# Two attention stages of a kernel: the uses of one shared PSUM bank get other places in the round

## What is computed

```python
x = x + _L0_ffn_ref(_layernorm(x), g_info, W_qkv, W_proj, b_proj)          # "ra": register attention
...
x = x + _L3_xattn_ref(ctx, _layernorm(x), mask, mask, W_src, ..., W_out)   # "ma": masked attention
```

## Time and profile before

| What | Value |
|---|---|
| median of three executions | 2350.74 us |
| the profiled execution, its own time | 2351.17 us |
| its span, granted TensorE clock | 2349.3 us, 0.959 |
| TensorE busy | 2057.0 us (88% of the span) |
| VectorE, ScalarE, GpSimd busy | 1252.7, 1019.3, 300.4 us |
| stage ra, 147 to 380 us of the span | 233.0 us, of it TensorE 212.76, VectorE 158.78, ScalarE 164.79 |
| stage ma, 1810 to 1987 us | 177.0 us, of it TensorE 165.50, VectorE 93.42, ScalarE 83.17 |

### The profile page before, as it was taken

One profiled execution on the slowest core, in us unless ns is written; L12 is line 12 of the kernel. 1 busy time (PEld: TensorE's weight loads), 2 busy tenths in 40 slices (PEclk: granted clock), 3 DMA queues, 4 the chain that ended last, 5 costly groups with the idle time before them and its releaser, 6 DMA issues. The chain is left out here.

```text
span 2349.3 us, 38236 instructions
## 1 busy us (share of the span) xinstructions
PE 2057.0 (88%) x14629; PEld 1545.4 (66%) x14629; DVE 1252.7 (53%) x2505; ACT 1019.3 (43%) x2851; POOL 300.4 (13%) x392
## 2 busy tenths in 40 slices
PE   6789998899997689979999999978998998785795
PEld 4556666566665589766666667657886777663684
DVE  6457665788876144365554455655444555553113
ACT  3247774777775245333333333443222544333122
POOL 0101110222211524200000000031002000001212
PEclk8989999999999889989999999999999999997898
DMA  3000001121212633340000000010002000005352
GB/s 132 18 1 1 1 2 46 28 56 38 58 33 90 234 85 90 99 148 10 10 10 10 1 10 1 1 32 1 1 1 79 28 19 22 1 1 167 126 184 81
DMA packets 92564, 114.79 MB, mean 49 GB/s; under 512 B 20217, under 2 KB 75521, under 8 KB 91489
## 3 DMA queue, kind: packets, MB, share of 16 engines
q1 hardware_dynamic: 87440, 98.75, 13.8%
q0 software_dynamic: 4944, 13.59, 1.6%
HBM read 79.89 MB, written 25.08 MB: 45 GB/s over the span
## 5 line engine op out<-in xcount | busy, mean ns | idle before, releaser
L957 ACT ACTIVATE ca_prob<-bank,ca_nmax 128x512 f32<-128x512 f32 x256 | 174.2, 691 | 73.2 <-DVE ca_nmax L1024 73.2
L1024 DVE TENSOR_REDUCE ca_nmax<-bank 128x1 f32<-128x512 f32 x256 | 164.2, 683 | 40.9 <-PE bank L806 40.9
L957 ACT ACTIVATE na_prob<-bank,na_nmax 128x257 f32<-128x257 f32 x256 | 118.1, 474 | 148.4 <-DVE na_nmax L1024 148.4
L820 PE MATMUL bank<-cst,ca_prob 128*128 128x128 f32 x1024 | 140.6, 278 | 7.6 <-DVE ca_pT L1030 5.9
L820 PEld LDWEIGHTS bank<-cst,ca_prob 128*128 128x128 f32 x1024 | 111.0, 141 | 53.6 <-issue 44.9
L957 ACT ACTIVATE ra_prob<-bank,ra_nmax 128x256 f32<-128x256 f32 x256 | 118.4, 486 | 53.4 <-DVE ra_nmax L1024 53.4
L1024 DVE TENSOR_REDUCE na_nmax<-bank 128x1 f32<-128x257 f32 x256 | 90.9, 418 | 68.7 <-PE bank L806 68.7
L2267 PE MATMUL bank<-sf_h,sf_W 128*128 128x512 f32 x512 | 120.1, 395 | 0.0
L2267 PEld LDWEIGHTS bank<-sf_h,sf_W 128*128 128x128 f32 x512 | 95.9, 187 | 23.5
L2135 PE MATMUL bank<-na_Wkv,na_cxT 128*128 128x512 f32 x224 | 103.6, 605 | 0.0
L1024 DVE TENSOR_REDUCE ra_nmax<-bank 128x2 f32<-128x512 f32 x128 | 82.0, 683 | 39.6 <-PE bank L806 39.6
(11 more groups left out here) (475 smaller groups left out, 4611.9 us busy)
## 6 DMA issues: line engine op xcount, KB each, us to landing
xl_w<-in_L_ffn_w SPq DMA_DIRECT2D x16, 1024.0 KB, 7.6
rf_sent<-rf_w SPq DMA_DIRECT2D x13, 390.0 KB, 6.2
rf_xin<-rf_sent SPq DMA_DIRECT2D x39, 128.0 KB, 2.1
dp_cx<-in_ctx_tok SPq DMA_DIRECT2D x4, 1024.0 KB, 13.8
ca_v<-in_ctx_values SPq DMA_DIRECT2D x8, 512.0 KB, 4.8
rf_W<-in_L_ffn_w SPq DMA_DIRECT2D x8, 512.0 KB, 10.6
rf_rows<-rf_back SPq DMA_DIRECT2D x8, 512.0 KB, 5.6
na_Wkv<-in_L_xattn_Wkv SPq DMA_DIRECT2D x1, 4096.0 KB
```

Source lines behind the costliest of these rows:

```text
L820: mm = pe.transpose(TB[f % 2][:, j * P:(j + 1) * P], prob[:, n % 2, u, c0:c0 + P], ident)
L957: e = act.activation(prob[:, n % 2, u, hh * keys:(hh + 1) * keys], S[u][:, hh * keys:(hh + 1) * keys], ACT.Exp, bias=nmax[:, n % 2, u, hh: ...
L1024: v.tensor_reduce(nmax[:, n % 2, u], S[u][:, 0:W].rearrange("p (h k) -> p h k", h=per), AX.X, ALU.max, negate=True).then_inc(maxed, 1)
```

## The change

Only the two tables `place` change. Every use is still issued once for each batch; none is added or removed.

```diff
@@ register_attention_layer
-                         place=[[[("last_reg", 3)], [("reg", 0)], []],
-                                [[], [("spread",)], []],
-                                [[("reg", 1)], [("project",)], [("front", 0)]],
-                                [[("front", 1)], [("reg", 2)], []]])
+                         place=[[[("last_reg", 2)], [], [("last_reg", 3)]],
+                                [[("reg", 0)], [("spread",)], []],
+                                [[("reg", 1)], [], [("project",)]],
+                                [[("front", 0)], [("front", 1)], []]])
@@ masked_attention_layer
                          late=(2,), place=[[[("front", 1)], [("project",)], [("front", 0)]],
-                                           [[("spread",)], [("front", 2)], []]])
+                                           [[("front", 2)], [("spread",)], []]])
```

## The result

The changed kernel takes 2363.06 us in the median of five executions (2360.84 to 2368.11), against 2350.74 before; the ratio of the two is 1.0059, with an interval of 1.0043 to 1.0076. So it is slower by 0.6%. The prediction had slower at 0.74 and 2358.3 us: 7.6 us of a move of 12.3 by the medians, or 13.9 by the ratio. Its range ended at 2364.5 us; the median lies inside it by 1.4 us, and the ratio on the median of before gives 2364.6. The profiled execution took 2368.11 us, the longest of the five, with a span of 2366.3 us: 17 more than before. From the first scores of ra to the first matmul of the layer norm behind it the two traces have 238.75 us (144.75 to 383.50) and 259.05 (143.40 to 402.45), +20.3. The same stretch of ma has 181.08 (1809.47 to 1990.55) and 179.05 (1831.87 to 2010.92), -2.0. The other stages together are 1.3 shorter.

The account below looks back on a forecast made before the run. TensorE was taken to set the batches of both stages, with a 6.32 us chain as floor of a round in ra. Ra +11.4 and ma -3.8 gave +7.6 us on 2351.17, so a median of 2358.3; range 2351 to 2364.5.

Parts of the forecast that it names:

- The removed wait: Round r=2 of ra: the projection's wait of 1.06 us goes, but TensorE then waits between the pairs; round 7.37 us.
- charged step 0 with 1.15: Round r=1 of ra: register step 0, moved there from r=0, adds four matmuls and a short mask, 1.15 us.
- So I charge nothing: Clock term in ra: new TensorE pauses up to 1.6 us in every batch leave the clock at 2.4 GHz; cost 0.
- the mechanism as a rival: Ra: the clock falls in each batch, 1.7 us a batch, 7 times 12 us in all: 2370 us; chance 0.05.
- The sign that I had named: Register stage: the prediction is wrong if the granted clock in the stage falls below 0.99.
- The first batch: Batch 0 of ra: step 0's exponential +0.5, round 2 loses the keys -0.6, round 3 +1.0; together +0.9 us.
- the steady gain: Ma: the waits of the spread (0.77 us) and of the keys (0.31) go; a batch of 22.0 us.
- round 1 loses: Round 1 of ma: the value projection leaves the gap between the pairs and stands a pair earlier; +2.7 us.
- The forecast of the cover: Ma: with VectorE's take of the values ahead, last mask at about 9.35 us, just covered by next scores at 9.49.
- the projection did not slide: Rival for r=2 of ra: bound by the exponentials only, 6.8 us; total 2354.8 us, within 0.2%; chance 0.15.
- the faster case: Rival in ra: TensorE's own work sets the batch, 25.9 us; decided by r=0 and r=2 together under 13.3; chance 0.09.
- the chain: Round r=0 of ra: scores to first maximum, first exponential and last mask, 1.29 + 0.73 + 4.30 = 6.32 us; no round shorter.

Follow-up runs that it names:

- experiment 4: Changed kernel plus useless matmuls in both short rounds of ra: seven in r=2, three between the pairs and two behind the second in r=0; 2355.66 us, ratio 1.0023.
- experiment 7: Changed kernel, but in the first batch of the register stage step 0 stays in round 0 as before; 2364.24 us, ratio 1.0053.
- ma alone: Kernel before with only the masked stage's table changed to the new one; 2345.02 us, ratio 0.9977.
- experiment 3: Changed kernel plus twelve useless 128-column matmuls between the two pairs of turns of r=2 in seven batches of ra; 2367.26 us, ratio 1.0075.

## Why the prediction was right or wrong

**The direction and the mechanism of the order were right.** Step by step, in us, from the batch at full clock (221.54, 228.80, 237.41, 244.30, 251.16):

| | before | forecast | after |
|---|---|---|---|
| r=2 | 8.56 | 7.37 | 7.26 |
| r=3 | 7.74 | 8.71 | 8.61 |
| r=0 | 6.32 | 7.00 | 6.89 |
| r=1 | 5.98 | 7.13 | 6.86 |
| batch | 28.60 | 30.21 | 29.62 |
| first maximum of r=0 | 1.29 | 1.97 | 1.87 |

The removed wait went and a longer one took its place, between the pairs, for the copies, as written. All four rounds came out 0.1 to 0.3 short, the most in r=1, where I charged step 0 with 1.15 and the round grew by 0.88. Step 0 did take 1.14 (245.27 to 246.41), but the scores ahead of it and the first pair behind it took 0.97 and 0.96 in place of 1.18 and 1.02. So six batches lost 6.1 us by the order, where I had +9.7.

**The step that failed is "So I charge nothing", on the clock.** It was a term of 0. In the profiled execution it measured 6.6 us in the six batches (experiment 4), another 1.7 in the last stretch (21.50 us from the seventh spread to the eighth, against 19.82 with the pauses filled), and about 3.3 ahead of the first spread (below): some 11.5 us. I had seen the mechanism as a rival and put it at 0.05, on the strength of a row in which TensorE is busy for 1.97 of 6.24 us with the clock at 1.00. That reads the pause. The fall comes behind it. The next 5 us of the same trace of before are

```profile
383.50:388.50 5.00, 5.00 (x64) 4.66 (x68) 1.51 (x2) 2.64 (x5) 1.81 (x2) 0.66 0.77 243
```

so the row that I gave as evidence against was evidence for, though for a stretch that is much emptier than the new pauses. The sign that I had named, a granted clock in the stage below 0.99, was no test: the whole stage reads 0.93 in the changed kernel but already 0.98 before, mostly for its first batch. The six steady batches tell them apart, 0.96 against 1.00. The price that I gave the rival, 1.7 us a fall, came out right (3.12 less 1.83 is 1.3 for the projection, 1.6 to 1.7 for the batch). The row behind it, though, is not 16 matmuls at the lower clock: the granted clock from 1810.66 to 1816.10 us is 0.69, so it holds one fall, of which the 1.7 us are the cost. The count was wrong: not in each of seven batches, but in four of six and in the last, and behind either of two pauses. The Trainium skill ("TensorE: Matmul & The Clock Gate", HAM oscillation) says that a loop whose matmuls pause in every turn can drop to half the clock again and again; its example waits 3 to 5 us for a transfer in each turn. The runs agree on the drops, where I had set them aside, and show them behind shorter pauses, 1.72 and 0.20 us in r=2: 0.95 granted in batches of 31.2 us, 1.00 with the pauses filled.

**The first batch** was forecast at +0.9. The stretch to the first spread holds r=0 and r=1 of the next batch too, so the forecast to set against it is 0.9 + 0.68 + 1.15 = 2.7. It grew by 6.6 (39.22 to 45.85), with the granted clock down from 0.90 to 0.80. By rounds, in the timelines: round 1 +1.6 (6.50 to 8.12), round 2 -0.6, round 3 +2.5 (7.73 to 10.23), r=0 +0.6, r=1 up to the spread +2.5 (4.99 to 7.50). In two of them the clock falls: it is 0.63 from 164.62 to 169.27 us, at the start of round 3, and 0.54 from 181.75 to 185.49, at the start of r=1. Each fall is 1.6 us: at full clock round 3 is 8.60 (experiment 7), and r=1 grows by 0.88. That makes 3.3 for the clock, 1.8 for the order of four rounds, and 1.6 for round 1, where I had 0.5 and where the traces don't part order from clock. The 3.3 that experiment 7 gave are round 1 and the fall in round 3.

**Ma:** the steady gain was right (22.0 forecast, 21.99), and that round 1 loses was right (2.7 forecast). The sum of -3.8 compares with -2.0 in the profiled stage and -5.4 by the ratio of the run with ma alone. Of the difference in the stage, 1.0 is round 0, in which nothing was moved: its first scores were at the full clock before and at half of it (0.50) in the changed kernel. Without it the stage is at -3.0. The forecast of the cover, last mask just under the next scores, held: that batch shows 21.80 us busy of 21.99.

**The sum.** Forecast +11.4 in ra and -3.8 in ma. The profile has +20.3 and -2.0. In ra the order was overcharged by 3.6 in the six batches and the clock left out: some 11.5 of the 20.3 are clock, and the order is 7 to 9 (6.1 in the six batches, 1.8 to 3.4 ahead of the first spread, -0.6 behind the seventh), against +11.4. So the direction was forecast for the right reason, and that 2358.3 us came no further off is partly luck, since the overcharged order covered part of the missing clock. Of the rivals, the projection did not slide (r=2 is 7.26, with the waits of the second pair in the trace), and the faster case failed since r=0 and r=2 together took 14.15 us, over its point of 13.3.

## What to carry to other kernels

A use that fills the gap between two dependent groups on TensorE is worth more than its own wait: ask what stands in the gap when it has left, and whether the round was bound by the chain or by work. Balance the rounds by the chain, not by the amount of work: a heavier long round costs its full work, while the short round gives nothing back below the chain. When a change adds pauses of TensorE, read the granted clock in the stretch behind comparable pauses of the old trace, not in the pauses themselves.

## What the runs showed of the hardware

The clock of a batch was not the same from one batch to the next with identical waits: up to the projection both show 3.5 us busy of 5.43 at 1.00, then the projection ran at 1.00 (2.4 GHz) in one and at 0.57 (1.2 GHz for most of it) in the other. Removing one pause did not remove the falls; they moved to the next one. Added matmuls of no use made the kernel faster: 72 more of them in six batches (144 instructions in the trace), and 6.6 us less. Whether it is the length of one pause that counts or how much of a stretch is idle, no run here separates; before, with a wait of 1.06 us in r=2, the clock of the steady batches did not fall. And 128-column float32 matmuls with the identity took about 0.22 us each (twelve in 2.68 us, experiment 3), where I had reckoned 0.12.
